# Dense products of a gated graph network: two float32r halves in place of three bf16 pieces

## The reference

```python
h = jnp.maximum(_layernorm(x, axis=-1), 0.0)
h = h @ lin_w.T + lin_b
for i in range(3):
    m = h @ weight[i]
    agg = jax.ops.segment_sum(m[src], dst, num_segments=n_nodes)
    h = gru_cell(agg, h, w_ih, w_hh, b_ih, b_hh)
return x + h
```

## Time and profile before

| | |
|---|---|
| median of 3 runs | 5407.77 us (5395.41 to 5431.67) |
| span of the profiled execution | 5300.9 us |
| PE, PE weight load, VectorE, ScalarE, POOL busy | 75%, 46%, 33%, 20%, 59% |
| dense matmuls (L778) | 11,172 |
| indirect gathers (L501) | 3,168 |
| mean DMA traffic | 195 GB/s |

### The profile page before, as it was taken

The page is one execution under the profiler, slowest core; times in us unless marked ns, Lnnn a source line. Parts: engine busy times, 40 slices in busy tenths (PEclk is TensorE's granted clock), DMA queues, the critical chain, the costliest instruction groups (busy, mean ns, idle before and its releaser), DMA issues.

```text
span 5300.9 us, 79449 instructions
## 1 busy us (share of the span) xinstructions
PE 3980.3 (75%) x28664; PEld 2446.9 (46%) x28665; DVE 1765.8 (33%) x7320; ACT 1082.1 (20%) x2162; POOL 3143.9 (59%) x3230
## 2 busy tenths in 40 slices
PE   5266666666667678885888888888848888889787
PEld 3144444444444444542454554545524544545454
DVE  7355555554555412221122222222212222222222
ACT  3044454544444400000000110101000000000000
POOL 4666566666566665644666566655556555566555
PEclk8587778777777789996899999989969989999899
DMA  5566666666666676674666666666746666666665
GB/s 194 156 182 179 174 180 180 181 178 175 175 176 181 178 238 204 220 223 150 199 214 207 220 208 212 203 203 203 244 149 203 214 195 207 204 212 215 191 213 161
DMA packets 748353, 1034.23 MB, mean 195 GB/s; under 512 B 89640, under 2 KB 622504, under 8 KB 747944
## 3 DMA queue, kind: packets, MB, share of 16 engines
q1 hardware_dynamic: 507288, 653.00, 37.6%
q0 software_dynamic: 152064, 311.63, 22.3%
q10 hardware_dynamic: 88592, 64.25, 3.9%
HBM read 797.45 MB, written 231.08 MB: 194 GB/s over the span
## 4 chain that ended last, share of the span: by engine, by line
PE 62%; issue 15%; another core or an unknown queue 12%; DVE 6%; ACT 2%; DVEq 1%; DMA 1%; POOL 0%; ACTq 0%; POOLq 0%; SPq 0%
PE psum L778 35%; PE psum L758 14%; PE psum L738 4%; PE psum L726 4%; DVE onehot L1057 1%; PE psum L698 1%; DVE pieces_region L1155 1%; PE psum L711 1%; DVE aggT L1095 1%; ACT stage_region L619 1%; PE psum L699 1%; DVEq L1047 1%; PE psum L700 1%; DVE pieces_region L882 0%
## 5 line engine op out<-in xcount | busy, mean ns | idle before, releaser
L501 POOL DMA_INDIRECT ring_region<-messages,edge_src x3168 | 3083.5, 973 | 2062.4 <-issue 918.8
L778 PE MATMUL psum<-stage_region,pieces_region 128*128 128x432 f16 x11172 | 2218.5, 354 | 191.2 <-issue 184.8
L778 PEld LDWEIGHTS psum<-stage_region,pieces_region 128*128 128x128 bf16 x11172 | 1089.0, 99 | 1243.2 <-issue 386.1
L758 PE MATMUL psum<-pieces_region,stage_region 128*128 128x238 bf16 (+2 forms) x5376 | 877.5, 323 | 505.8 <-issue 351.2
L1081 DVE TENSOR_TENSOR aggT<-aggT,psum 128x36 f32 x792 | 152.7, 193 | 2653.1 <-remote 1501.5
L758 PEld LDWEIGHTS psum<-pieces_region,stage_region 128*128 128x128 bf16 x5376 | 579.2, 118 | 789.9 <-issue 621.5
L619 ACT CAST stage_region<-psum 128x504 f16<-128x504 f32 x1344 | 737.1, 586 | 677.7 <-PE psum L758 313.4
L738 PE MATMUL psum<-onehot,ring_region 128*128 128x36 bf16 x9504 | 361.8, 182 | 375.2 <-issue 316.4
L557 ACT ACTIVATE temps<-psum,small 128x256 f32<-128x256 f32 x147 | 69.8, 475 | 2385.3 <-PE psum L726 1635.9
L738 PEld LDWEIGHTS psum<-onehot,ring_region 128*128 128x128 bf16 x9504 | 328.9, 99 | 452.3 <-issue 403.8
L1057 DVE TENSOR_SCALAR onehot<-iota_block,edge_rel 128x36 bf16<-128x36 bf16 x3168 | 479.0, 249 | 2.4 <-issue 2.3
(11 more groups left out here) (97 smaller groups left out, 1324.4 us busy)
## 6 DMA issues: line engine op xcount, KB each, us to landing
stage_region<-counts SPq DMA_DIRECT2D x532, 768.0 KB
counts<-stage_region SPq DMA_DIRECT2D x1344, 128.0 KB
ring_region<-messages,edge_src POOLq DMA_INDIRECT x3168
pieces_region<-messages SPq DMA_DIRECT2D x24, 1344.0 KB
messages<-pieces_out ACTq DMA_DIRECT2D x98, 192.0 KB
temps<-states ACTq DMA_DIRECT2D x98, 128.0 KB
states<-temps ACTq DMA_DIRECT2D x98, 128.0 KB
messages<-ring_region SPq DMA_DIRECT2D x25, 384.0 KB, 2.8
```

The costliest lines, as they stand in the source:

```text
L501: nc.gpsimd.indirect_dma_start(out=rows[:, n % RING, h * QC + c, :], out_offset=None, in_=messages[layer], in_offset=bass.IndirectOffsetOn ...
L758: mm = nc.tensor.matmul(by_block[:, :, SUBLOW[c]:SUBLOW[c] + SUBW[c]], blocks_oh[j % 2][:, c, :], x_round, start=(k == 0), stop=True, skip ...
L778: mm = nc.tensor.matmul(psum[:, 6 + kg % 2, 0:DQ * W], res[:, b, piece * P:(piece + 1) * P], stage[v % ABUF][:, :, cols], start=(b == 0 an ...
```

## The change

A message is now kept resident as plain fp32, one value in place of three pieces. Before a dense block is multiplied, its seven-block slice is prepared on the chip: VectorE makes a *high half* (the fp32 value converted to float32r) and a *low half* (the value less the high half, again float32r), and ACT widens the slice of counts from fp16 to float32r. A dense block is then two float32r matmuls. Both new buffers exist twice (`UBUF` = 2): slice v is made once slice v-2 has been used. `ABUF` falls from 4 to 3, and SP refills a buffer once ACT has widened what was in it. The gathered path keeps its three bf16 pieces and its 768-byte rows.

To have fp32 messages to load, each tile also copies its messages to an fp32 tile (ACT, L631 of the new code) and stores them in a new array `plain` (128 KB a tile); the same is done for layer 0 in the prologue, 25 copies of 128x512 and 25 stores of 256 KB. The resident messages are loaded seven times 0.9 MB a layer, and once more after the counts are built, since the build's scratch lies in the same region. In the prologue `aggT` is lent to other buffers and zeroed later, and the queue memory of the indirect DMA is set to 8192 bytes.

```diff
@@ SP @@
-            def pieces_in(layer, i):
+            def messages_in(layer, i):
                 sp.dma_start(res[:, 2 * HB * i:2 * HB * (i + 1), :],
-                             tile_rows(messages[layer], 2 * HB * P * i, 2 * HB * P)).then_inc(s_res[i], 16)
+                             tile_rows(plain[layer], 2 * HB * P * i, 2 * HB * P)).then_inc(s_res[i], 16)
...
                 k = DENSE_OF[0][used] if used < KD else (used - KD) % NSB
+                if v >= ABUF:
+                    sp.wait_ge(s_wide, v - ABUF + 1)
                 sp.dma_start(stage[v % ABUF], counts[k, j]).then_inc(s_al[v % ABUF], 16)
...
+            messages_in(0, 0)
             for v in range(KD * SLICES):
-                if v == ABUF:
-                    for i in range(HELD, PARTS):
-                        pieces_in(0, i)
-                slice_used(v - ABUF)
+                if 1 <= v < PARTS:
+                    messages_in(0, v)
                 counts_in(v)
@@ PE @@
                 if b % HB == 0:
-                    pe.wait_ge(s_al[v % ABUF], 16 * (v // ABUF + 1))
-                if k == 0 and b % (2 * HB) == 0:
-                    pieces_loaded(layer, b // (2 * HB))
+                    pe.wait_ge(s_wide, v + 1)
+                    pe.wait_ge(s_low, v + 1)
...
-                for piece in range(PIECES):
-                    mm = nc.tensor.matmul(psum[:, 6 + kg % 2, 0:DQ * W], res[:, b, piece * P:(piece + 1) * P],
-                                          stage[v % ABUF][:, :, cols], start=(b == 0 and piece == 0),
-                                          stop=(b == NB - 1 and piece == PIECES - 1))
+                for half in range(HALVES):
+                    mm = nc.tensor.matmul(psum[:, 6 + kg % 2, 0:DQ * W],
+                                          halves[:, v % UBUF, b % HB, half * P:(half + 1) * P],
+                                          wide_counts[:, v % UBUF, :, cols], start=(b == 0 and half == 0),
+                                          stop=(b == NB - 1 and half == HALVES - 1))
@@ VectorE @@
+            def split(layer, v):
+                used, j = v // SLICES, v % SLICES
+                if used == DENSE0[layer] and j % 2 == 0:
+                    dve.wait_ge(s_res[j // 2], 16 * (layer + 2))
+                slice_used(dve, v - UBUF)
+                whole = res[:, HB * j:HB * (j + 1), :]
+                high, low = (halves[:, v % UBUF, :, half * P:(half + 1) * P] for half in range(HALVES))
+                nc.vector.tensor_copy(high, whole).then_inc(s_high, 1)
+                dve.wait_ge(s_high, v + 1)
+                nc.vector.tensor_tensor(low, whole, high.bitcast(F32), ALU.subtract).then_inc(s_low, 1)
+
             def layer_steps(layer, tiles_at):
                 for s in all_steps(layer, tiles_at):
                     n = STEP0[layer] + s
+                    for v in SLICES_AT_HEAD.get((layer, s), ()):
+                        split(layer, v)
@@ ScalarE @@
+                for v in SLICES_AT_HEAD.get((layer, s), ()):
+                    widen(v)
                 if s - 2 in tiles_at:
                     top_piece(layer, tiles_at[s - 2])
                 if s in tiles_at:
                     gates(layer, tiles_at[s])
 
             def step_end(layer, tiles_at, s):
+                for v in SLICES_AT_TAIL.get((layer, s), ()):
+                    widen(v)
```

More of the change, by code:

```diff
@@ L51 @@
 F16 = mybir.dt.float16
+F32R = mybir.dt.float32r
 DVE_E = mybir.EngineType.DVE
@@ L57, with gated_graph_layers @@
 ON_CHIP = "the plan is made on the chip from node numbers below the number of rows"
[L60 removed]
+def gated_graph_layers(nc, x, src, dst, lin_wT, lin_b, weight, w_ihT, w_hhT, b_ih, b_hh, out, messages, plain, states,
+                       counts):
     NPAD = x.shape[0]
@@ new lines, in gated_graph_layers @@
+        keys = f32_at(region, DI0, DC)
+        los = f32_at(region, DI0 + 4 * DC, DC)
+        split_i = i32_at(region, EX0, DC)
+        XB = NB * sum(SUBW) * 2
+        xs = [[half_at(region, b * XB + NB * sum(SUBW[:c]) * 2, NB * SUBW[c], BF16)
+               for c in range(QC)] for b in range(2)]
+        iota_x = half_at(region, 2 * XB, XIOTA, F16)
+        LO0 = 2 * XB + 2 * XIOTA
+        blocks_oh = [half_at(region, LO0 + b * QC * P * 2, QC * P, BF16
+                             ).rearrange("p (c w) -> p c w", w=P) for b in range(2)]
@@ L300, in gated_graph_layers @@
         s_p30 = sem("first_messages_low_piece")
+        s_p320 = sem("first_messages_whole")
+        s_plain0 = [sem(f"first_whole_messages_stored_{s}") for s in range(PRO)]
         s_h0T = [sem(f"h0_stored_{s}") for s in range(PRO)]
@@ L1159, in counting_buffers @@
             def counting_buffers():
-                for i in range(HELD, PARTS):
+                for i in range(PARTS):
                     dve.wait_ge(s_res[i], 16)
@@ L1198, in layer_steps @@
                             quad_onehot(j)
-                    for i in range(len(DENSE_OF[layer])):
-                        if superblock_step(layer, i) == s:
-                            add_superblock(layer, i, s)
                     if s in tiles_at:
                         gate_n(layer * NT + tiles_at[s])
+                    ended = [i for i in range(len(DENSE_OF[layer])) if superblock_step(layer, i) == s]
+                    for v in SLICES_AT_TAIL.get((layer, s), ()):
+                        while ended and (DENSE0[layer] + ended[0] + 1) * SLICES <= v:
+                            add_superblock(layer, ended.pop(0), s)
+                        split(layer, v)
+                    for i in ended:
+                        add_superblock(layer, i, s)
             for layer in range(LAYERS):
@@ L1258 @@
                         for i in range(LAYERS)]
+    args["plain"] = [nc.dram_tensor(f"plain_{i}", (tiles if i else whole, D), F32, kind="Internal").ap()
+                     for i in range(LAYERS)]
     args["states"] = nc.dram_tensor("states", (P, whole), F32, kind="Internal").ap()
```

179 lines of the change are left out of this document (107 added, 72 removed).

## The result

The changed kernel takes **5491.64 us** (median of 7 runs, 5456.29 to 5500.66), the kernel before 5425.40 in the same comparison (7 runs, 5395.41 to 5441.93). The ratio is 1.0116, 95% interval 1.009 to 1.0142: **slower by 1.2%**, 66 us. I had said 5347.

A forecast was written before the change was run, and what follows sets the result against it. PE is busiest, but POOL's run of eight gathers plus its pause paces a step. Pace -104, gathers +27, prologue +10, reload +7 make -60: span 5241, plus 106.9 to the median, 5347 us; eight-in-ten range 5080 to 5600.

The forecast's parts named there:

- The price of a float32r matmul: Dense products on PE: each float32r matmul taken as 0.20 us, bounds 196 and 392 ns, so 5.7 us a step.
- Rival 3: Dense products on PE: float32r matmuls run at half rate, 392 ns each, giving 5620 to 6150 us; chance 0.09.
- The sizes of the new operations: Per slice: widening 2.73 us on ScalarE; subtraction 1.09 us and copy 0.5 to 1.09 us on VectorE.
- The pace, -104 us: Dense steps: late PE steps vanish, 12.59 becomes 12.2 us over 266 steps, -104 us (bounds 0 and -186).
- The two levels, 12.2 and 12.59: Dense steps: 12.2 us when no late PE lengthens one, 12.59 us as read from the profile before the change.
- The coupling with POOL, +27 us: POOL's gathers beside more VectorE work: 0.1 us a step longer (bounds 0 and 0.54), 266 steps, +27 us.
- Prologue and reload, +17 us: Prologue copies and stores +10 us (0 to 30); loading whole messages again after the build +7 us (0 to 30).
- It hides behind 12.2: ScalarE's 6.7 us and VectorE's 6.3 to 7.4 us of work a step fit within the 12.2 us step.
- Rival 2: Dense steps: waits between slice making and PE's late news idle PE; steps 12.9 to 13.2 us, 5540 to 5600; chance 0.14.
- the new work has a whole step of slack for one of two buffers: The prediction's argument against the rival of a new chain through two slice buffers, which had chance 0.14.

The follow-up runs named there:

- e1: The kernel before with only the indirect DMA's queue memory set to 8192 bytes; 5401.0 us, ratio 0.9976.
- e9: The changed kernel without widenings and splits from the third slice on, and without the waits for them; 5316.1 us, ratio 0.9796 to the kernel before.
- e11: As e9, with the stale slices in fp16 (counts) and bf16 (halves) in place of float32r; 5321.8 us, ratio 0.9801 to the kernel before.
- e4: The changed kernel with the low half made by a plain copy in place of the subtraction; 5454.5 us, ratio 1.0061 to the kernel before.
- e3: The changed kernel with widening and split shrunk to one or eight columns from the third slice on, all waits kept; 5403.9 us, ratio 0.9963 to before.

## Why the prediction was wrong

The forecast was -60 us, the measured difference is +66. The prediction's steps, one by one:

- *The price of a float32r matmul, 0.20 us, bounds 0.196 and 0.392.* Nearer the lower bound, but a fifth too low: 702.36 us for 2845 of them in the window of layer 1 are 0.247 us at a granted clock of 0.83, where e1 has 0.198 at 0.92 for its own. In long runs of matmuls the timelines show 0.207 to 0.22 us each after (here 0.215), and 0.186 before:

```profile
3211.84 4.30 PE L834 MATMUL psum<-wide_counts,message_halves 128*128 128x432 f32 x20
```

```profile
3169.06 7.83 PE L778 MATMUL psum<-stage_region,pieces_region 128*128 128x432 f16 x42
```

  Rival 3 (half rate) is out. The Trainium skill ("FP8 and Floating Point Precision", TensorE Precision Notes) names a mode that reads 4-byte fp32 and truncates it, beside four passes for true fp32; the 0.215 us against 0.186 agree with no added pass. That the price was low mattered little: e9 and e11 differ by 6 us.
- *The sizes of the new operations.* 2.73 us forecast for the widening, 2.715 measured; 1.09 for the subtraction, 1.093; 0.5 to 1.09 for the copy, 1.080.
- *The pace, -104 us.* Right as a difference when tested nearly by itself: e9, the change without its slices and the waits for them, is 2.0% (111 us) below before, and its step is 12.44 us against 12.80 in e1, 0.36 less where I had 0.39. The two levels, 12.2 and 12.59, were both too low, and it is partly luck that their difference held.
- *The coupling with POOL, +27 us.* Wrong in size as busy time: 1.054 us a gather against 0.949 in e1 (783.20 for 825) is 0.84 us a step, over my upper bound of 0.54. The build stage was probably a poor row for it, since 565 of the 599 us of its VectorE work (in e1) are TENSOR_SCALAR operations, another kind than the subtraction; that was not tested. As a price it is small: 37 us with two buffers (e4), nothing that shows with four. The Trainium skill ("SBUF — State Buffer", SBUF: two separate sides) warned of a hold, for an issued gather by the fp32 copy, and for an operation with two SBUF inputs only against a GpSimd operation that reads SBUF. Here the copy from fp32 to float32r holds nothing and the operation with two SBUF inputs does.
- *Prologue and reload, +17 us.* The first gather starts at 124.5 us against 127.3 in e1, and the first dense product starts 16.8 us after the last product of the build against 13.3: about nil.
- ***"It hides behind 12.2", for ScalarE and for VectorE: the step that failed.*** I compared busy times with the length of a step, 6.7 and 6.3 to 7.4 against 12.2, and costed the wait that the change adds at nothing. But the later products of a step now need operations that stand behind the adds of that step in VectorE's queue, and in a locked step these start only when POOL pauses. That costs 88 us for the wait alone (e9 to e3) and 88 for the operations' length, in VectorE's queue and, through the middle piece, in ScalarE's (e3 to after). The sum -111 + 88 + 88 = +65 must come to about the measured 66, as these are the steps from before over e9 and e3 to after; it says how the loss divides and is no further test.

Rival 2, which I gave 0.14, is near to what happened. It had the late news, the idling in mid-step and the step (12.9 to 13.2 us, measured 13.13), and it left out VectorE's queue and the middle piece. I had put it about 50 us too dear, because I took its step against 12.59 us, which came from a quick execution; 12.80 is the usual one, and 0.21 us over 266 steps are 56 us. What spoke against it, "the new work has a whole step of slack for one of two buffers", was argued and not read: the earlier trace rows had shown that VectorE itself starts late in a step.

## What to carry to other kernels

A new stage between a DMA and the busiest engine is not free because its engines have time: ask which queue it stands in, what is at that queue's head, and how many buffers lie between. Where the head waits for a late event once a step, as here, two buffers of half a step's work each were too few; test the depth with operations shrunk to nothing before costing the operations. And take the reference for a stage from an execution whose span agrees with the timed runs.

## What the runs showed of the hardware

- A VectorE operation with two SBUF inputs (fp32, 128x896, 1.09 us) holds an indirect gather of POOL that starts beside it: in the case shown it ends 0.82 us after the operation and takes 1.76 us in place of 0.95. A cast of the same size, fp32 to float32r (1.08 us), doesn't.
- A float32r weight load of 128x128 takes 216 ns on average (after) against 99 to 102 for bf16 (before, e11), and a matmul of 432 columns takes 0.207 us with it in its fastest long runs against 0.186.
- Queue memory for indirect DMAs of 8192 bytes in place of the default costs nothing for these gathers of 128 rows: 5401 us against 5416 for before on the same chip (ratio 0.9976, 0.9953 to 1.0).
